# A decoder layer on one core: six tile banks, stepwise output products and a third norm by halves for the last chunk

## The chip, the cores and the metric

The kernel runs on one core of one Trainium2 chip. The metric is the device time of one execution in microseconds (us). TensorE (PE in the profile) multiplies matrices into PSUM, which has eight banks; VectorE (DVE), ScalarE (ACT) and GpSimd (POOL) do elementwise work; SyncE (SP) issues most DMA transfers. Engines run their own instruction lists in order and wait for each other on semaphores.

## The reference

The input is `x`, 16 sequences of 256 tokens of width 256, and a context of the same shape. Three sublayers follow each other, each as `x = layernorm(x + sublayer(x))`:

1. A recurrent attention: an input projection, a causal convolution over four steps, gates, cosine and sine of scaled values, a running sum over the tokens, a normalisation by head and an output projection.
2. An autocorrelation attention over the context: Fourier transforms of queries, keys and values, the five strongest lags by a softmax, the values shifted by those lags, an output projection.
3. A mixture of 8 experts in two branches:

```python
xV = einsum('btd,kdr->btkr', Q_side, V)
yW = einsum('btd,kdr->btkr', K_side, W)
prod = xV * cumsum(yW, axis=1)
weights = softmax(gelu(Q_side @ router_w1.T + b1) @ router_w2.T + b2)
out = einsum('btkr,kdr->btd', prod * weights[..., None], U) + weights @ b
out = out / n_valid[None, :, None]
```

The two branches are added, one with a factor, multiplied by `W_O`, and the third layer norm ends the layer.

## The kernel before

The 16 sequences are worked off in 8 chunks of two (512 tokens, four row blocks `q` of 128). Each chunk goes through three stages, named by their first letter: `a_...`, `b_...` and `c_...` are the steps of sublayers 1, 2 and 3. Every step is a small function on each engine that takes part in it, and every engine has a list of calls, written out in order, in which steps of up to three neighbouring chunks are interleaved: while chunk `i` is in stage a, chunk `i-1` is in b and `i-2` in c. The last chunk's stage c therefore runs alone. Before the first chunks, and among them, 34 `fold(k)` steps on PE and ACT combine weights.

PSUM banks are divided among the stages: 0 to 2 for a, 3 and 4 for b, 5 to 7 for c (`BANK_A`, `BANK_B`, `BANK_C`). Before a step writes a bank, `free_c` makes PE wait until the bank's former contents are read.

Stage c works over `NJ` = 8 expert tiles `j`. For each, `c_running(j)` (bank 5), `c_own(j)` (bank 6) and `c_spread(j)` (bank 7) are products on PE of nine instructions together; ACT copies the first to `cs`; DVE multiplies it by the spread weights (`c_scale`, L2810) and by the own product (`c_prod`, L2818), which gives `prod[:, j]`. When all eight are there, `c_out(n)` for each half `n` of the row blocks multiplies `prod` by `up` (L797) and adds the bias (L798): 64 instructions and 4. DVE adds the residual for each half and takes statistics (`c_residual`, L2827, L2608), aggregates them for all four row blocks after the second half (L2614); POOL makes scale and offset (`rstd`, L2309 to L2314, the `pow` in L2312), ACT applies them (`c_layer`, L1651) and writes into a part of `prod`, and SP stores the chunk (L371, 512 KB).

On PE, `a_factor(i, h)` (L557) needs `pair` from a chain over DVE and ACT that begins with `a_squares(i)` (L605). `b_transform` is L637, `b_wt` L674, `b_wf` L685, `a_project` L576, `a_sums` L593, `fold` L436 and L453; `a_conv` on DVE is L2490. SP's loads wait for PE steps: `load_residual(i)` for `b_transform(i-1, "xf", 1)`.

## Time and profile before

| | |
|---|---|
| three runs | 960.15, 957.73 and 961.58 us, median 960.15 |
| profiled execution | 960.6 us, span of its trace 958.7 us |
| PE busy | 865.2 us, 90% of the span |
| DVE busy | 766.4 us, 80% |
| ACT busy | 537.6 us, 56% |
| POOL busy | 96.2 us, 10% |
| mean granted TensorE clock | 0.957 of 2.4 GHz |

The span runs from the first to the last instruction or transfer of the profiled execution. The granted clock is the share of full speed that TensorE was given. An engine's busy share is a mean over the whole span.

### The profile page before, as it was taken

Reading aid. Unit: us, or ns where it says so; the run is one execution under the profiler, and the core shown is the slowest. Engines: PE = TensorE matmul, PEld = TensorE weight load, DVE = VectorE, ACT = ScalarE, POOL = GpSimd, SP = SyncE. Lnnn points to the kernel's source line nnn. Section 1 sums busy time; section 2 is a strip of 40 time slices with the busy share of each in tenths; the row PEclk is TensorE's granted clock in tenths of the full one; section 3 lists DMA queues with packets and bytes.
Section 4 is the critical chain, followed back from the end, with each engine's and each line's share of the span. In section 5 each row is a group of like instructions: output and inputs, shape, how many; then the busy total and the mean of one; then the engine's idle time right before and its main releaser. Section 6 shows DMA issues by size and latency. Waiting matters only on the chain.

```text
span 958.7 us, 11672 instructions
## 1 busy us (share of the span) xinstructions
PE 865.2 (90%) x4056; PEld 510.3 (53%) x4056; DVE 766.4 (80%) x1290; ACT 537.6 (56%) x875; POOL 96.2 (10%) x174
## 2 busy tenths in 40 slices
PE   3569865999999999999999999999999999997896
PEld 1134633663665556564756466555655475656345
DVE  5796888989878999899979997899879995373231
ACT  3484892677448673767467755856475655311310
POOL 2010011300120011100210011100200021001000
PEclk9679996999999999999999999999999999999898
DMA  9742034110432024100611044001510150000000
GB/s 292 133 89 44 6 83 88 46 45 0 83 72 67 0 48 85 66 23 13 120 45 45 1 91 107 23 0 35 120 44 1 23 111 23 1 1 23 0 1 22
DMA packets 41214, 50.81 MB, mean 53 GB/s; under 512 B 14843, under 2 KB 34374, under 8 KB 41158
## 3 DMA queue, kind: packets, MB, share of 16 engines
q0 software_dynamic: 7008, 25.21, 13.9%
q1 hardware_dynamic: 34006, 24.48, 8.9%
q8 instruction: 33, 0.54, 0.2%
q10 hardware_dynamic: 144, 0.39, 0.1%
q14 instruction: 23, 0.19, 0.1%
HBM read 20.68 MB, written 4.19 MB: 26 GB/s over the span
## 4 chain that ended last, share of the span: by engine, by line
PE 71%; DVE 18%; ACT 6%; issue 3%; POOL 1%; DMA 1%; ACTq 0%; DVEq 0%; SPq 0%; POOLq 0%
PE ps L797 12%; PE ps L778 10%; PE ps L769 9%; PE ps L653 6%; PE ps L593 5%; PE ps L735 5%; PE ps L576 4%; DVE sc L2569 3%; PE ps L623 3%; PE ps L712 3%; PE ps L637 3%; DVE zc L2490 2%; PE ps L436 2%; DVE sc L2561 2%; PE ps L702 2%
## 5 line engine op out<-in xcount | busy, mean ns | idle before, releaser
L2569 DVE TENSOR_TENSOR_SCAN sc<-mask,sc 128x1024 f32<-128x1024 bf16 x64 | 146.2, 2284 | 0.4
L778 PE MATMUL ps<-x2t,mv 128*128 128x512 f32 x256 | 123.7, 606 | 0.3 <-DVE prod L2818 0.3
L769 PE MATMUL ps<-cum,mw 128*128 128x512 f32 x256 | 122.1, 599 | 0.3 <-ACT cs L1646 0.2
L797 PE MATMUL ps<-up,prod 128*128 128x256 f32 x512 | 115.6, 381 | 1.3 <-DVE prod L2818 1.2
L797 PEld LDWEIGHTS ps<-up,prod 128*128 128x128 f32 x512 | 94.7, 190 | 18.9 <-issue 4.8
L2325 POOL DMA_DIRECT2D acc<-sq x48 | 42.1, 877 | 567.9 <-ACT sq L1552 567.9
L1646 ACT ACTIVATE cs<-ps 128x512 f32<-128x512 f32 x64 | 38.0, 594 | 99.8 <-PE ps L769 95.0
L2561 DVE TENSOR_TENSOR sc<-sc,g 128x1024 f32<-128x1024 f32 x64 | 77.3, 1208 | 7.4 <-ACT sc L1536 7.3
L2490 DVE SCALAR_TENSOR_TENSOR zc<-ps,cst,zc 128x510 f32<-128x510 f32 (+2 forms) x96 | 71.3, 742 | 13.7 <-ACT zc L1463 11.4
L769 PEld LDWEIGHTS ps<-cum,mw 128*128 128x128 f32 x256 | 47.4, 191 | 63.6 <-issue 59.5
L593 PE MATMUL ps<-sc,wy 64*64 64x512 f32 x512 | 66.1, 638 | 10.9 <-DVE sc L2569 10.9
L778 PEld LDWEIGHTS ps<-x2t,mv 128*128 128x128 f32 x256 | 47.0, 191 | 52.0 <-issue 44.1
L1552 ACT ACTIVATE sq<-sc 128x1024 f32<-128x1024 f32 x48 | 50.5, 1051 | 39.2 <-DVE sc L2569 22.9
L576 PE MATMUL ps<-xt,win 128*128 128x512 f32 x128 | 64.9, 636 | 7.1 <-DVE zc L2490 7.1
L2810 DVE TENSOR_TENSOR cs<-cs,ps 128x512 f32<-128x512 f32 x64 | 43.5, 679 | 30.2 <-ACT cs L1646 17.2
L735 PE MATMUL ps<-x2t,mr 128*128 128x512 f32 x128 | 59.3, 614 | 0.8 <-ACT x2t L1606 0.8
L1399 ACT ACT_TABLE_LOAD x45 | 57.7, 1283 | 2.0 <-PEq L3514 1.2
L2818 DVE TENSOR_TENSOR prod<-cs,ps 128x512 f32<-128x512 f32 x64 | 43.7, 683 | 12.6 <-PE ps L778 11.5
L1518 ACT ACTIVATE hq<-zc,cst 128x512 int32<-128x512 f32 x64 | 45.9, 719 | 7.4 <-DVE zc L2490 6.2
L2541 DVE SCALAR_TENSOR_TENSOR frac<-zc,cst,hq 128x512 f32<-128x512 f32 x64 | 47.5, 745 | 1.1 <-ACT hq L1518 0.7
L1536 ACT ACTIVATE sc<-hq,quarter 128x512 f32<-128x512 f32 x64 | 45.4, 709 | 0.0
L1651 ACT ACTIVATE prod<-x,rsc 128x256 f32<-128x256 f32 x32 | 16.6, 588 | 48.8 <-POOL rsc L2314 48.8
(263 smaller groups left out, 1478.1 us busy)
## 6 DMA issues: line engine op xcount, KB each, us to landing
acc<-sq POOLq DMA_DIRECT2D x48, 512.0 KB, 4.6
xa<-in_x_dram SPq DMA_DIRECT2D x8, 512.0 KB, 4.4
xs_a<-in_x_dram SPq DMA_DIRECT2D x8, 512.0 KB, 3.6
cin<-in_ctx_dram SPq DMA_DIRECT2D x8, 512.0 KB, 4.6
out_dram<-prod SPq DMA_DIRECT2D x8, 512.0 KB, 3.0
win<-in_in_proj_dram SPq DMA_DIRECT2D x1, 544.0 KB, 6.6
prod<-in_L_ffn_V_fwd_dram SPq DMA_DIRECT2D x2, 256.0 KB
prod<-in_L_ffn_W_fwd_dram SPq DMA_DIRECT2D x2, 256.0 KB
```

The lines of the kernel that those rows point to most:

```text
L576: last = mm(o, win[:, t, j * P:(j + 1) * P], xt[:, t, :], start=(t == 0), stop=(t == DT - 1))
L593: last = mm(ps[dst, BANK_A[("Y", r)], :], wy[src, 1 - c, m, :], sc[src, (2 * m + h) % 4, c, :], start=(m == 0 and c == 0), stop=(m == M - ...
L653: last = mm(o[:, b * D:(b + 1) * D], spec[:, first + t, c:c + P], w[:, t, :], start=(t == 0), stop=(t == DT - 1 and not biased))
L735: last = mm(o, mr[:, t, br, r * P:(r + 1) * P], x2t[:, t, :], start=(t == 0), stop=(t == 1))
L769: last = mm(o, mw[:, t, br, c:c + P], cum[:, t, :], start=(t == 0), stop=(t == 1))
L778: last = mm(o, mv[:, t, br, c:c + P], x2t[:, t, :], start=(t == 0), stop=(t == 1))
L797: mm(d, prod[:, j, q * P:(q + 1) * P], up[:, j, :], start=(j == 0), stop=False)
L1399: act.preload_act_table_set(name)
L1552: A(dst, sc[:, u % 4, :, :], ACT.Square, scale=1.0 / math.sqrt(2.0 * HD * M))\
L2490: STT(o[:, :, s:L], z[:, :, 0:L - s], cw[:, j, tap:tap + 1], o[:, :, s:L], ALU.mult, ALU.add)\
L2561: TT(sc[:, s, :, :], sc[:, s, :, :], g[:, h, :].unsqueeze(1).broadcast_to([P, 2, T]), ALU.mult)\
L2569: V.tensor_tensor_scan(flat, mask[:, 0:2 * T], flat, 0.0, ALU.mult, ALU.add)\
```

## The change

For the last chunk alone, the expert tiles alternate between two sets of three banks: 5, 6, 7 for even `j` and 3, 4, 2 for odd `j` (`BANK_LAST`); its outputs stand in banks 0 and 1. A new step `c_last(j)` adds tile `j`'s part to all four output blocks, for `j` from 0 to 6; `c_out` then does only tile 7 and the bias. `c_last(7, 0)` stands behind `c_spread(7, 1)`, the other six behind the last `c_own`.

For all chunks the third norm is done by halves: aggregates behind each half of the residual, `c_rstd(i, n)` on POOL, `c_layer(i, n)` on ACT and two stores of 256 KB. A few semaphores are merged under common names, with the same waits (`pr`, `ws`). Finally the lists of calls of PE, ACT, DVE and SP are in another order in many places of all chunks. The diff, cut to its core:

```diff
-POOL_C = Steps("pool_c", each("rstd", range(4)))
+POOL_C = Steps("pool_c", each("rstd", range(8)))
...
+BANK_LAST = dict(BANK_C)
+for _j in range(1, NJ, 2):
+    BANK_LAST.update({("c", _j): 3, ("x", _j): 4, ("w", _j): 2})
+BANK_LAST.update({("out", 0): 0, ("out", 1): 1})
...
-            def store(i):
-                sp.wait_ge(*ACT_C.at(i, "norm", NQ - 1))
-                sp.dma_start(rows(out, i), xs_c[:, :, :]).then_inc(stored, 16)
+            def store(i, n):
+                sp.wait_ge(*ACT_C.at(i, "norm", 2 * n + 1))
+                sp.dma_start(rows(out, i)[:, 2 * n:2 * n + 2, :], xs_c[:, 2 * n:2 * n + 2, :]).then_inc(stored, 16)
...
-            store(3)
+            store(3, 0)
+            store(3, 1)
+            load_x(7)
             load_ctx(6)
-            load_x(7)
+            store(4, 0)
+            store(4, 1)
             load_residual(6)
-            store(4)
             load_residual(7)
...
             def free_c(i, *name):
-                prev, i = before(BANK_C, i, name)
-                if prev is None:
-                    return ps[:, BANK_C[name], :]
+                bank = bank_c(i)[name]
+                o = ps[:, bank, :]
+                mine = [g for g in bank_c(i) if bank_c(i)[g] == bank]
+                n = mine.index(name)
+                if n:
+                    prev = mine[n - 1]
+                elif is_first(i) or bank < 5:
+                    return o
+                else:
+                    prev, i = [g for g in BANK_C if BANK_C[g] == bank][-1], i - 1
...
+            def accumulate(o, q, j, start):
+                return mm(o[:, (q % 2) * D:(q % 2 + 1) * D], prod[:, j, q * P:(q + 1) * P], up[:, j, :], start=start, stop=False)
+
+            @staged
+            def c_last(i, j):
+
+                o = [free_c(i, "out", n) for n in range(2)] if j == 0 else [ps[:, bank_c(i)[("out", n)], :] for n in range(2)]
+                pe.wait_ge(*VEC_C.at(i, "prod", j))
+                for q in range(NQ):
+                    last = accumulate(o[q // 2], q, j, j == 0 and q % 2 == 0)
+                last.then_inc(*PE_C.tick("last", j))
+
             @staged
             def c_out(i, n):
-                o = free_c(i, "out", n)
+                o = ps[:, bank_c(i)[("out", n)], :] if is_last(i) else free_c(i, "out", n)
                 pe.wait_ge(*VEC_C.at(i, "prod", NJ - 1))
                 if is_first(i):
                     pe.wait_ge(placed, 16 * PARTS)
                 for q in range(2 * n, 2 * n + 2):
-                    d = o[:, (q % 2) * D:(q % 2 + 1) * D]
-                    for j in range(NJ):
-                        mm(d, prod[:, j, q * P:(q + 1) * P], up[:, j, :], start=(j == 0), stop=False)
-                    last = mm(d, wparts[:, q * P:(q + 1) * P], bp3[:, 0, :], start=False, stop=True)
+                    for j in (range(NJ - 1, NJ) if is_last(i) else range(NJ)):
+                        accumulate(o, q, j, j == 0)
+                    last = mm(o[:, (q % 2) * D:(q % 2 + 1) * D], wparts[:, q * P:(q + 1) * P], bp3[:, 0, :], start=False,
+                              stop=(q % 2 == 1 or not is_last(i)))
                 last.then_inc(*PE_C.tick("out", n))
...
-            fold(0)
             a_project(0, 3)
             a_sums(0, 0)
+            fold(0)
             fold(1)
-            a_sums(0, 1)
             fold(2)
             fold(3)
             fold(4)
             fold(5)
             fold(6)
+            a_sums(0, 1)
             fold(7)
...
             b_transform(0, "cf", 0)
             b_transform(0, "cf", 1)
+            a_project(1, 3)
             b_transform(0, "xf", 0)
             b_transform(0, "xf", 1)
-            a_project(1, 3)
             b_spectrum(0, "qa")
...
+            c_last(7, 1)
+            c_last(7, 2)
+            c_last(7, 3)
+            c_last(7, 4)
+            c_last(7, 5)
+            c_last(7, 6)
             c_out(7, 0)
             c_out(7, 1)
...
-            def c_layer(i):
-                ln_apply(i, 2, x2, xs_c, ACT_C, POOL_C)
+            def c_layer(i, n):
+                if n == 0 and not is_last(i):
+                    act.wait_ge(*PE_C.at(i, "out", 1))
+                act.wait_ge(*POOL_C.at(i, "rstd", 4 * n + 3))
+                for q in range(2 * n, 2 * n + 2):
+                    A(xs_c[:, q, :], x2[:, q, :], ACT.Identity, bias=rs[2][:, 2, q:q + 1], scale=rs[2][:, 1, q:q + 1])\
+                        .then_inc(*ACT_C.tick("norm", q))
...
+            @staged
+            def c_rstd(i, n):
+
+                q, sums = slice(2 * n, 2 * n + 2), rs[2]
+                pool.wait_ge(*VEC_C.at(i, "aggr", 2 * n + 1))
+                G.tensor_tensor(sums[:, 0, q], mvr[2][:, q, 1], eps_[:, q], ALU.add).then_inc(*POOL_C.tick("rstd", 4 * n))
+                G.tensor_tensor(sums[:, 2, q], mvr[2][:, q, 0], minus[:, q], ALU.mult).then_inc(*POOL_C.tick("rstd", 4 * n + 1))
+                pool.wait_ge(*POOL_C.at(i, "rstd", 4 * n + 1))
+                G.tensor_tensor(sums[:, 1, q], sums[:, 0, q], half_[:, q], ALU.pow).then_inc(*POOL_C.tick("rstd", 4 * n + 2))
+                pool.wait_ge(*POOL_C.at(i, "rstd", 4 * n + 2))
+                G.tensor_tensor(sums[:, 2, q], sums[:, 2, q], sums[:, 1, q], ALU.mult).then_inc(*POOL_C.tick("rstd", 4 * n + 3))
...
                 ln_stats(i, 2, x2, VEC_C, n)
-                if n == 1:
-                    ln_aggr(i, 2, VEC_C)
+                dve.wait_ge(*VEC_C.at(i, "stats", 2 * n + 1))
+                V.tensor_copy(seen[:, 2:3], st[2][:, 2 * n, 0:1])
+                for q in range(2 * n, 2 * n + 2):
+                    V.bn_aggr(mvr[2][:, q, :], st[2][:, q, :]).then_inc(*VEC_C.tick("aggr", q))
```

Other moves in the lists that matter below: on PE folds 20 and 21 go from before `a_factor(0, 0)` to behind `a_project(1, 1)`; between `b_wt(1)` and `b_wf(1)`, neighbours before, four steps are put; in chunk 3 `b_out(2, 1)` goes from before to behind `a_factor(3, 0)`; in chunk 4 `b_transform(4, "cf", 0)` goes from before to behind `a_factor(4, 0)`; in chunk 6 the order `a_squares`, `b_transform(6, "cf", 0)`, `a_factor(6, 0)` becomes `a_squares`, `b_out(5, 1)`, `a_factor(6, 0)`, `b_transform(6, "cf", 0)`. On ACT folds are moved as well: fold 0 to behind `a_turns(0, 6)`, folds 8 and 9 before `a_angles(0, 7)`, fold 10 behind it. On DVE `b_fold(0, "xf")` goes from behind `a_conv(1, 1)` to behind `a_conv(1, 2)`.

## Rows read from the trace of the kernel before

**Rows 1.** The page, busy us by engine (share of the span) x instructions.
```profile
PE 865.2 (90%) x4056; PEld 510.3 (53%) x4056; DVE 766.4 (80%) x1290; ACT 537.6 (56%) x875; POOL 96.2 (10%) x174
```

**Rows 2.** Windows: stretch, length, busy us of each engine, granted clock, DMA share, GB/s.
```profile
168.00:880.00 712.00, 696.70 (x3354) 417.85 (x3351) 611.98 (x1037) 417.92 (x672) 75.03 (x128) 0.99 0.20 45
880.00:907.50 27.50, 17.96 (x49) 7.84 (x48) 6.47 (x19) 12.27 (x20) 1.64 (x5) 0.81 0.06 19
907.50:933.80 26.30, 26.19 (x64) 11.34 (x64) 10.32 (x15) 4.58 (x8) 0.00 (x0) 1.00 0.00 1
933.80:949.30 15.50, 14.50 (x68) 12.24 (x68) 2.37 (x6) 0.00 (x0) 0.00 (x0) 1.00 0.00 0
949.30:958.70 9.40, 0.00 (x0) 0.00 (x0) 2.01 (x9) 2.07 (x4) 1.56 (x4) 0.62 0.17 56
```

**Rows 3.** Timeline of the end: start, us, engine, instruction, [idle before it <- releaser].
```profile
908.77 0.69 DVE L2818 TENSOR_TENSOR prod<-cs,ps 128x512 f32<-128x512 f32 x1
909.78 0.38 PE L786 MATMUL ps<-wparts,sel 128*128 128x512 bf16 x1
...
933.88 0.69 DVE L2818 TENSOR_TENSOR prod<-cs,ps 128x512 f32<-128x512 f32 x1 [0.68 <-PE ps L778]
934.71 3.69 PE L797 MATMUL ps<-up,prod 128*128 128x256 f32 x16 [0.94 <-DVE prod L2818]
...
949.24 0.88 DVE L2827 SCALAR_TENSOR_TENSOR x<-ps,cst,x 128x256 f32<-128x256 f32 x2 [5.47 <-PE ps L798]
951.01 0.37 DVE L2614 BATCH_NORM_AGGREGATE mvrc<-stc 128x2 f32<-128x6 f32 x4
951.46 0.20 POOL L2309 TENSOR_TENSOR rsc<-mvrc,eps_ 128x4 f32<-128x4 f32 x1 [67.67 <-DVE mvrc L2614]
951.89 1.01 POOL L2312 TENSOR_TENSOR rsc<-rsc,half_ 128x4 f32<-128x4 f32 x1
953.21 2.07 ACT L1651 ACTIVATE prod<-x,rsc 128x256 f32<-128x256 f32 x4 [20.74 <-POOL rsc L2314]
955.31 0.37 SPq L371 DMA_DIRECT2D out_dram<-prod  x1
```

**Rows 4.** DMA issues: tensors, queue, count, KB each, median us to landing.
```profile
out_dram<-prod SPq DMA_DIRECT2D x8, 512.0 KB, 3.0
bp<-bp POOLq DMA_DIRECT2D x2, 16.0 KB, 1.9
```

**Rows 5.** PE's waits, 185 to 880 us: us in total, times, longest us.
```profile
PE ps L557 <- DVE pair L2590: 2.8, 2, 2.4
...
PE ps L637 <- DVE cin L2635: 1.9, 1, 1.9
PE ps L685 <- ACT wtt L1594: 1.2, 1, 1.2
...
PE ps L769 <- ACT cs L1646: 0.2, 1, 0.2
```

**Rows 6.** Timeline of PE at two of these waits.
```profile
240.37 1.05 PE L685 MATMUL ps<-wtt,fdft 128*128 128x32 f32 x8 [1.24 <-ACT wtt L1594]
...
796.34 0.47 PE L557 MATMUL ps<-pair,spreads 128*128 128x256 f32 x2 [2.37 <-DVE pair L2590]
```

**Rows 7.** Windows of 4 us behind these two waits, columns as in rows 2.
```profile
240.00:244.00 4.00, 3.63 (x12) 2.21 (x13) 2.66 (x8) 0.71 (x3) 0.95 (x1) 0.70 0.58 112
...
798.00:802.00 4.00, 4.00 (x16) 3.36 (x15) 1.54 (x3) 2.48 (x3) 0.00 (x0) 0.58 0.00 0
```

**Rows 8.** Timeline of the start: PE and DVE.
```profile
55.47 3.69 PE L593 MATMUL ps<-sc,wy 64*64 64x512 f32 x16 [10.70 <-DVE sc L2569]
...
115.07 2.29 DVE L2490 SCALAR_TENSOR_TENSOR zc<-ps,cst,zc 128x510 f32<-128x510 f32 x3
117.76 1.88 PE L576 MATMUL ps<-xt,win 128*128 128x512 f32 x4
120.49 2.31 DVE L2490 SCALAR_TENSOR_TENSOR zc<-ps,cst,zc 128x510 f32<-128x510 f32 x3 [3.13 <-ACT zc L1463]
```

More of the change, by code:

```diff
@@ L832, in _ @@
             fold(19)
+            a_sums(0, 2)
             a_sums(0, 3)
             a_squares(0)
-            fold(20)
-            fold(21)
             a_factor(0, 0)
@@ L909, in _ @@
             b_transform(1, "xf", 1)
+            a_spread(2, 1)
+            a_project(2, 2)
             c_weights(0)
-            a_project(2, 2)
-            c_spread(0, 0)
             b_spectrum(1, "qa")
@@ L931, in _ @@
             c_spread(0, 4)
-            a_sums(2, 0)
+            b_wt(1)
             c_own(0, 4)
@@ L936, in _ @@
             c_own(0, 5)
+            b_wf(1)
             c_running(0, 6)
             c_spread(0, 6)
-            b_wt(1)
-            b_wf(1)
             c_own(0, 6)
             c_running(0, 7)
-            a_sums(2, 1)
+            a_sums(2, 0)
             c_spread(0, 7)
             c_own(0, 7)
+            a_sums(2, 1)
             b_back(1)
@@ L992, in _ @@
             c_running(1, 2)
+            a_sums(3, 0)
             c_spread(1, 2)
@@ L1008, in _ @@
             c_spread(1, 6)
+            a_sums(3, 1)
             c_own(1, 6)
-            b_wt(2)
             c_running(1, 7)
             c_spread(1, 7)
+            b_wt(2)
             c_own(1, 7)
@@ L1046, in _ @@
             a_spread(4, 1)
+            a_project(4, 2)
             c_own(2, 0)
@@ L1138, in _ @@
             c_running(3, 4)
+            a_sums(5, 0)
+            b_wt(4)
             c_spread(3, 4)
-            b_wt(4)
             c_own(3, 4)
             c_running(3, 5)
+            b_wf(4)
             c_spread(3, 5)
-            b_wf(4)
             c_own(3, 5)
@@ L1170, in _ @@
             a_scores(6)
+            a_project(6, 0)
             a_out(5, 1)
+            c_transpose(4, 0)
+            c_transpose(4, 1)
+            a_project(6, 1)
             c_hidden(4, 0)
-            a_project(6, 0)
-            a_project(6, 1)
             c_hidden(4, 1)
@@ L1194, in _ @@
             b_spectrum(5, "vb")
+            c_own(4, 0)
+            c_weights(4)
             a_project(6, 3)
+            c_spread(4, 0)
             c_running(4, 1)
+            a_sums(6, 0)
+            b_corr(5)
             c_spread(4, 1)
@@ L1212, in _ @@
             c_spread(4, 5)
+            b_wf(5)
             c_own(4, 5)
@@ L1215, in _ @@
             c_spread(4, 6)
-            b_wf(5)
+            a_sums(6, 1)
             c_own(4, 6)
@@ L1225, in _ @@
             a_sums(6, 2)
+            a_sums(6, 3)
             b_out(5, 0)
+            a_squares(6)
             b_out(5, 1)
-            a_sums(6, 3)
-            a_squares(6)
+            a_factor(6, 0)
             b_transform(6, "cf", 0)
-            a_factor(6, 0)
             b_transform(6, "cf", 1)
             a_factor(6, 1)
+            a_transpose(7, 0)
+            a_transpose(7, 1)
+            a_out(6, 0)
+            a_scores(7)
+            a_out(6, 1)
+            a_project(7, 0)
             c_transpose(5, 0)
             c_transpose(5, 1)
-            a_transpose(7, 0)
-            a_out(6, 0)
-            a_transpose(7, 1)
-            a_out(6, 1)
-            a_scores(7)
-            a_project(7, 0)
             a_project(7, 1)
@@ L1268, in _ @@
             c_own(5, 1)
+            a_sums(7, 0)
             c_running(5, 2)
@@ L1271, in _ @@
             c_own(5, 2)
-            a_sums(7, 0)
             c_running(5, 3)
-            b_wt(6)
             c_spread(5, 3)
@@ L1277, in _ @@
             c_running(5, 4)
+            c_spread(5, 4)
+            b_wt(6)
+            c_own(5, 4)
             b_wf(6)
-            c_spread(5, 4)
-            c_own(5, 4)
             c_running(5, 5)
@@ L1367, in _ @@
             c_spread(7, 1)
+            c_last(7, 0)
             c_own(7, 1)
@@ L1697, in _ @@
             a_turns(0, 6)
-            a_squares(0, 2)
-            a_angles(0, 5)
-            a_turns(0, 7)
-            a_squares(0, 3)
+            fold(0)
             fold(1)
@@ L1704, in _ @@
             fold(3)
+            a_squares(0, 2)
+            a_angles(0, 5)
             fold(4)
@@ L1708, in _ @@
             fold(7)
+            a_turns(0, 7)
+            a_squares(0, 3)
             a_angles(0, 6)
@@ L1943, in _ @@
             a_project(4, 0)
+            a_project(4, 1)
+            b_transform(3, "cf", 0)
             c_hidden(2, 0)
-            a_project(4, 1)
-            a_turns(4, 0)
-            b_transform(3, "cf", 0)
             c_hidden(2, 1)
@@ L2085, in _ @@
             a_scores(6)
+            b_layer(4)
+            b_transform(5, "cf", 0)
+            b_transform(5, "cf", 1)
             a_exp(6)
             a_project(6, 0)
+            c_transpose(4, 0)
+            c_transpose(4, 1)
             c_hidden(4, 0)
+            a_project(6, 1)
             a_layer(5)
-            a_project(6, 1)
             c_hidden(4, 1)
@@ L2892, in _ @@
             a_conv(1, 2)
+            b_fold(0, "xf")
             a_conv(1, 3)
@@ L3303, in _ @@
             a_den(7)
+            b_fold(6, "xf")
             a_conv(7, 1)
```

681 lines of the change are left out of this document (345 added, 336 removed).

## The prediction

> **What bounds the kernel now.** I read the page's busy shares first [rows 1]: TensorE (PE) is busy for 865.2 of 958.7 us, VectorE (DVE) for 766.4. A share is an average over stages, so I cut the span into stretches [rows 2]. From 168 to 880 us, where chunks overlap, PE is busy 696.70 of 712 us and DVE 611.98: there PE sets the pace, and 15.3 us of its time are open. From 880 to 907.5 us the last chunk is alone; PE works 17.96 of 27.5 us at a mean granted clock of 0.81, waiting for a chain of norm, gates and softmax. Then come the last chunk's expert tiles, 907.5 to 933.8 us, with PE busy 26.19 of 26.3 us; the output products, 14.50 us of PE work in a stretch of 15.5 us; and 9.4 us with no PE work at all. The rows of the end [rows 3] show one gap of 0.94 us, where PE waits for the last `prod`, and behind the last product a serial chain: residual and statistics on DVE, four small operations on POOL, four activations on ACT (2.07 us), one store.
>
> The profiled execution took 960.6 us, 1.9 us more than its span and 0.45 us more than the median of the three runs (960.15). The sum is made against 960.6 us, and its result shifted by that 0.45 us.
>
> **Six tile banks.** With three banks the next tile's products must wait until ACT or DVE has read the bank. In this stretch they do not: the 26.19 of 26.3 us leave 0.11 us for all waits [rows 2]. Alternating banks 5, 6, 7 with 3, 4, 2 therefore gains between nothing and 0.1 us; I take nothing. What hides the reads is the time that PE takes for a tile: 64 instructions at nine a tile are seven tiles, 3.7 us each, against two DVE operations of 0.69 us [rows 3]. The banks below 5 were used by chunk 7's first two stages, which are over before.
>
> **Output products as tiles come.** The same 64 product and 4 bias instructions are issued in another order; at 14.50 us for all, a bias counting half, a product instruction is 0.22 us [rows 2]. `c_last(7, 0)` stands behind `c_spread(7, 1)` and needs `prod` 0, which DVE ends at 908.77 + 0.69 = 909.46 us, while the spread begins only at 909.78 us [rows 3]: it does not wait. It pushes what is behind it by eight instructions, 1.8 us, which come off the end again. `c_last(7, 1)` to `c_last(7, 6)` stand behind the last tile's own product; their `prod` tiles are made by then, and their 48 instructions, 10.5 us, cover the 0.94 us in which PE waited for `prod` 7 [rows 3]. PE's last product ends 0.94 us earlier, at about 948.2 us. If that cover failed, the cost is the same 0.94 us.
>
> **Third norm and store by halves.** Since all outputs grow in step, the first half is ready only 1.1 us before the second: four products and two biases, five times 0.22 us. That is 947.1 us. DVE takes for the second half with all four aggregates from 949.24 to 951.01 + 0.37 = 951.38 us, 2.14 us [rows 3], and two aggregates less are 0.18 us less: 1.96 us a half. Half 0 keeps DVE until 949.1 us, so half 1 begins then and not at 948.2 us when PE is done, and ends at 951.05 us against 951.38. Of the 0.94 us, 0.6 are given back: the split makes DVE the queue at the end. This item is -0.3 us.
> POOL's four operations reach from 951.46 to 953.2 us, of them the `pow` on four columns 1.01 us [rows 3]. No row shows one on two columns: its cost lies between 0.5 us (by columns) and 1.01 us (all fixed). Its neighbours need 0.20 us for as many numbers, so most of any such operation is fixed; I take 1.01 us and no gain. Half 0 leaves POOL at 950.9 us, before half 1 comes. ACT then has two activations behind POOL's last result where it had four: 2.07 us become 1.05, a gain of 1.0 us.
> The last store carries 256 KB, not 512. From its issue at 955.31 us to the end of the span are 3.4 us [rows 3], 3.0 of them landing; a copy of 16 KB took 1.9 us [rows 4]. Half the data lies between 1.9 and 3.0 us; half way it is 2.45 us, a gain of 0.55 us. SP's issue of the first half's store (0.37 us) lies beside ACT's work, 2 us ahead.
> In the other seven chunks the halves cost one more copy and one more wait on DVE (0.15 us), four more POOL operations and one more issue on SP. DVE has 100 us open between 168 and 880 us [rows 2], so some 1 us for seven chunks is hidden; if DVE were the bound it would be paid.
> The tail's sum is -0.3 - 1.0 - 0.55 = -1.85 us. Its bounds are -2.9 us (short `pow`, 1.9 us landing) and -1.0 us (only ACT's part comes).
>
> **The lists of calls.** The diff also moves calls on every engine in all chunks; most of the uncertainty is here.
> In the start folds 2 to 6 move into PE's wait of 10.70 us before the second `a_sums(0, ...)` [rows 8]. What ends these stages is DVE's and ACT's work, so shorter PE queues pay little, and ACT's copies move too: fold 10 comes behind `a_angles(0, 7)` and holds PE's `mv` folds back. I take nothing for both. A later place pays: `a_project(1, 3)` moves ahead of the two `xf` transforms, and `b_fold(0, "xf")` into DVE's 3.13 us idle behind `a_conv(1, 2)`. PE may begin the projection when that convolution ends, at 115.07 + 2.29 = 117.36 us, not at 117.76 [rows 8]. I take -0.6 us for the start, with -3.1 us (the whole idle) and +2 us (the later copies) as ends.
> In the middle PE has 13.9 us of waits in 14 groups, of which four are shown, the first and the last among them [rows 5]. Two can be pointed at: `b_wt` and `b_wf` of chunk 1 stood next to each other (1.2 us) and get four steps between them, and `b_transform(6, "cf", 0)` waited 1.9 us for the fold of `cin` and now stands behind `b_out(5, 1)` and `a_factor(6, 0)`. Together -3.1 us. Against that, in chunks 3 and 4 less work stands before `a_factor`, which waits on a chain over DVE and ACT: 2.4 us where nothing fills it [rows 6]. And `load_residual(6)` now queues on SP behind both stores of chunk 4; if it came late, `a_residual(6, 0)` would hold PE. I take +2.1 us for these, -1.0 us together, with -7 us (half the waits go) and +6 us as ends.
> A wait costs more than its length. In the four microseconds that hold the end of the 1.2 us wait the granted clock is 0.70, and behind the wait of 2.4 us it is 0.58, so PE spent part of them at 1.2 instead of 2.4 GHz [rows 6, 7]. The second took 0.42 of 4 us, 1.7 us, beside the gap. Over 712 us the mean clock of 0.99 is some 7 us [rows 2].
> The Trainium skill (TensorE: Matmul & The Clock Gate, HAM oscillation) says that it is long idle gaps of TensorE that throttle it. By that rule gaps of one or two microseconds cost only their length, and the first rival below would end at 962.5 us, no measurable change; the trace does not agree, with its 0.58 behind a gap of 2.4 us, and the measurement decides.
>
> **Sum.** 960.6 - 1.85 - 0.6 - 1.0 = 957.15 us for the profiled execution, 956.7 as a median: I say 957.
>
> **Rivals.**
> A, slower: new gaps at the seams between chunks, where `a_factor` waits for DVE's `pair`. One more gap like that of chunk 7 costs 2.4 + 1.7 = 4.1 us [rows 6, 7], and two of them 8.2 us: 960.15 - 2.45 + 8.2 = 966 us. It decides from two gaps on. For it: chunk 4 has nothing left between `a_squares` and `a_factor`. Against: chunk 4 waited there before as well, and chunk 6 gets a filler. 0.09.
> B, clearly better lists: half of the middle's 13.9 us of waits and half of its 7 us of clock go, 10.5 us, less 3 us of new ones; the start gives twice its 0.6 us. With the tail it is 960.15 - 7.5 - 1.2 - 1.85 = 949.6 us. For it: the two waits above go with their clock. Against: PE is at 97.9% there already. 0.21.
> C, the change does not do what it says: queueing at DVE takes the whole 0.94 us, the store lands no sooner, and the lists cancel out; 959.2 us. For it: 0.6 us are given back in my own sum. 0.18.
> My forecast has 0.52, with 954 to 960 us as its own range.
>
> **How the numbers follow.** About 0.5% (4.8 us) is what a measurement of this kernel can tell from no change: faster begins below 955.35 us, slower above 964.95. Faster gets B and the lower edge of the forecast (0.09), 0.30; slower gets nearly all of A, 0.08; no change the rest, 0.62. The range cuts off A and half of B: 951.5 to 962 us.
>
> **What would show it.** 56 product instructions in one run behind the last tile, without a gap before `c_out(7, 0)`; the second half's residual starting when DVE is free, not when PE is done; two activations behind POOL's last result; a last store that lands in about 2.45 us; PE's end 8.6 us before the span's, where it was 9.5. In the middle PE's waits sum to 11 to 15 us. I am wrong if that sum is below 8 or above 18 us, if the first `c_transpose` moves by over 2 us, or if the first `c_last` waits.

## The result: 0.9% faster, and the profile after

The changed kernel took 951.16 us (median of five executions) against 961.28 us for the kernel before beside it, a ratio of 0.9913 with a 95% interval of 0.9889 to 0.9937. A second timing on another occasion gave 952.25 against 959.41 us, 0.9926 [0.9907, 0.9945]. Both are faster by more than the 0.5% bound. The forecast was 957 us: the first median lies 0.3 us below the low end of its range, the second inside it, and both are below the forecast's own range of 954 to 960. The prediction had put 0.62 on no measurable change and 0.30 on faster. One execution each of `tail_only`, `lists_only` and `after_order` below took 2009 to 2288 us; the ratios leave them out.

The page of after begins with its span and the busy shares:

```profile
span 948.8 us, 11724 instructions
PE 858.4 (90%) x4056; PEld 507.4 (53%) x4056; DVE 767.0 (81%) x1298; ACT 538.2 (57%) x876; POOL 106.4 (11%) x206
```

PE is busy for 6.8 us less than before with the same products [rows 1]. Next, the windows of after, columns as in [rows 2]:

```profile
180.00:872.00 692.00, 676.70 (x3293) 405.48 (x3292) 601.70 (x1020) 415.78 (x666) 79.86 (x146) 1.00 0.20 45
...
899.80:926.10 26.30, 26.29 (x70) 12.56 (x71) 9.63 (x14) 4.48 (x8) 0.00 (x0) 1.00 0.00 1
926.10:940.00 13.90, 13.89 (x64) 11.09 (x62) 2.40 (x5) 0.06 (x1) 0.00 (x0) 1.00 0.00 0
940.00:948.80 8.80, 0.00 (x0) 0.00 (x0) 2.74 (x12) 2.18 (x4) 2.48 (x8) 0.68 0.18 60
```

The first window of [rows 2] begins 12 us earlier in the work, at 168 us. The stretch of before that has the same 3293 instructions of PE is this:

```profile
180.00:879.00 699.00, 684.16 (x3293) 409.43 (x3292) 601.07 (x1013) 413.50 (x663) 70.05 (x118) 0.99 0.20 44
```

The middle has 15.3 us without PE work after (692.00 - 676.70) and 14.8 us before (699.00 - 684.16). The waits have not gone, they have moved. The three largest groups of waits between 180 and 875 us, by line (busy, mean ns, idle time ahead and its releasers):

```profile
L765 PE MATMUL ps<-x2t,mr 128*128 128x512 f32 x112 | 49.8, 593 | 1.6 <-ACT prod L1663 1.6
...
L667 PE MATMUL ps<-fdft,cin 128*128 128x128 f32 x112 | 14.6, 277 | 1.5 <-DVE x L2826 1.5
...
L587 PE MATMUL ps<-pair,spreads 128*128 128x256 f32 x48 | 12.4, 339 | 7.5 <-DVE pair L2672 4.7 <-issue 1.8 <-DVE zc L2680 0.8
```

L587 is the old L557: now two factor spreads, those of chunks 4 and 7, wait 2.4 us each, where one did [rows 5, 6]. So one of the two new waits that rival A asked for did come, in chunk 4. What is different is the clock behind such waits. These are the windows of after that hold the two waits of 2.4 us:

```profile
476.00:480.00 4.00, 1.63 (x15) 0.99 (x14) 2.95 (x11) 1.81 (x5) 2.35 (x4) 1.00 0.00 0
480.00:484.00 4.00, 3.57 (x28) 3.24 (x27) 2.55 (x4) 2.60 (x6) 0.00 (x0) 1.00 0.02 6
788.00:792.00 4.00, 1.88 (x15) 1.83 (x16) 3.26 (x7) 3.22 (x7) 0.80 (x2) 1.00 0.01 3
792.00:796.00 4.00, 3.25 (x17) 2.52 (x16) 3.85 (x5) 2.37 (x3) 0.00 (x0) 1.00 0.00 0
```

The granted clock is 1.00 behind both, where before had 0.58 behind the same wait [rows 7]. The end of after, the rows that answer to [rows 3] (PE's weight loads left out):

```profile
927.29 10.96 PE L819 MATMUL ps<-up,prod 128*128 128x256 f32 x50
...
939.72 0.27 PE L839 MATMUL ps<-bp,wparts 128*128 128x256 bf16 x1
...
940.71 0.24 DVE L2915 BATCH_NORM_AGGREGATE mvrc<-stc 128x2 f32<-128x6 f32 x2
940.86 0.84 DVE L2909 SCALAR_TENSOR_TENSOR x<-ps,cst,x 128x256 f32<-128x256 f32 x2
...
942.60 0.24 DVE L2915 BATCH_NORM_AGGREGATE mvrc<-stc 128x2 f32<-128x6 f32 x2
942.92 0.20 POOL L2372 TENSOR_TENSOR rsc<-mvrc,eps_ 128x2 f32<-128x2 f32 x1 [0.50 <-DVE mvrc L2915]
...
943.34 0.70 POOL L2375 TENSOR_TENSOR rsc<-rsc,half_ 128x2 f32<-128x2 f32 x1
...
944.35 1.09 ACT L1721 ACTIVATE prod<-x,rsc 128x256 f32<-128x256 f32 x2 [0.80 <-POOL rsc L2377]
```

The products run in one piece, without a wait for the last `prod`. PE ends at 939.99 us; the second half's residual starts only at 940.86 us, when DVE has finished the first half. Behind POOL's last result stand two activations. From PE's end to the span's end are 8.8 us, where there were 9.5.

What ends last is no longer the store. The page's row for the stores (KB each, median us to landing) and the closing instructions of after, each with its duration in ns and its start in us:

```profile
out_dram<-prod SPq DMA_DIRECT2D x16, 256.0 KB, 2.1
...
L186 POOLq EVENT_SEMAPHORE  x2: 17/17/17, 948.6 to 948.7; - x2
...
L186 POOLq DRAIN  x1: 4479/4479/4479, 944.1 to 944.1; - x1
...
L186 SPq COMPARE_BRANCH  x1: 33/33/33, 947.6 to 947.6; - x1
```

and the same instructions of before:

```profile
L171 POOLq EVENT_SEMAPHORE  x2: 17/17/17, 958.5 to 958.6; - x2
...
L171 POOLq DRAIN  x1: 4482/4482/4482, 952.9 to 952.9; - x1
...
L171 SPq COMPARE_BRANCH  x1: 33/33/33, 958.3 to 958.3; - x1
```

The `COMPARE_BRANCH` is the end of SyncE's wait for the last landing; the `DRAIN` closes GpSimd's list and begins at the end of its `pow`. Before, the drain was over at 957.42 us and the store landed at 958.27 us, so the store came last. After, the store landed at 947.61 us and the drain was over only at 948.56 us, so the drain came last. The other profiles agree: in all seven with the whole store the span ends 0.39 us behind the landing, in all six with halves 0.24 us behind the drain.

### The profile page after: what moved, and what is told of

Read it like the earlier page. It is cut to its first block, busy times and chain, and to the rows that moved or that the text cites. A ratio compares the mean times of both kernels' runs of the same rounds, so it can differ in the third digit from the quotient of the medians.

```text
span 948.8 us, 11724 instructions
## 1 busy us (share of the span) xinstructions
PE 858.4 (90%) x4056; PEld 507.4 (53%) x4056; DVE 767.0 (81%) x1298; ACT 538.2 (57%) x876; POOL 106.4 (11%) x206
## 4 chain that ended last, share of the span: by engine, by line
PE 72%; DVE 17%; ACT 6%; issue 3%; DMA 1%; POOL 1%; ACTq 0%; DVEq 0%; SPq 0%; POOLq 0%
PE ps L819 12%; PE ps L808 10%; PE ps L799 10%; PE ps L683 7%; PE ps L623 5%; PE ps L765 5%; PE ps L606 4%; PE ps L653 3%; DVE sc L2651 3%; DVE zc L2572 2%; PE ps L742 2%; PE ps L667 2%; PE ps L732 2%; DVE sc L2643 1%; PE ps L774 1%
## 5 line engine op out<-in xcount | busy, mean ns | idle before, releaser
L808 PE MATMUL ps<-x2t,mv 128*128 128x512 f32 x256 | 121.8, 598 | 0.2 <-DVE prod L2900 0.2
L606 PEld LDWEIGHTS ps<-xt,win 128*128 128x128 f32 x128 | 24.2, 204 | 35.4 <-issue 22.2
```

What stands on the lines that cost most here:

```text
L606: last = mm(o, win[:, t, j * P:(j + 1) * P], xt[:, t, :], start=(t == 0), stop=(t == DT - 1))
L808: last = mm(o, mv[:, t, br, c:c + P], x2t[:, t, :], start=(t == 0), stop=(t == 1))
```

## The experiments

Each kernel was timed beside the kernel before on the same chip, whose median in the three batches was 959.74, 959.41 and 959.34 us. PE runs a 128x256 product call of fp32 as two instructions of 0.22 us, so a filler call is 0.44 us.

### One part at a time

`tail_only` is the changed kernel with the lists of before: every call that both have stands where it stood before.

```diff
             c_spread(7, 1)
+            c_last(7, 0)
...
             c_own(7, 7)
+            c_last(7, 1)
...
+            c_last(7, 6)
             c_out(7, 0)
...
-            store(7)
+            store(7, 0)
+            store(7, 1)
```

> The kernel before with the change's last chunk alone: six banks, output products as tiles come, third norm and stores by halves in all chunks; the calls that both versions share stay in the order of before. Theory one (the tail and the lists are separate items, the tail worth what the two profiles show from the first last-chunk spread to the end of the span, 51.14 against 48.99 us): 2.1 us faster than before, a ratio of 0.998, with the low granted clock at 240 and 798 us still there. Rival (the halves, through two stores and more operations in every chunk, are what keeps the clock up in the middle): 8 to 10 us faster, ratio 0.990 to 0.992, and no low clock in the middle.

`lists_only` is the reverse: the structure of before with the order of after.

> The kernel before with the lists of calls of after alone: three banks, output products at the end, third norm and store whole. Theory one: the lists are worth the 7.1 us by which the middle is shorter in the profile of after, plus 0.7 us of clock in the first hidden products of the last chunk: 7 to 8 us faster, ratio 0.992, the middle without low granted clock. Rival: with the tail as before nearly nothing of it comes, under 3 us, ratio over 0.997.

`tail_only` took 957.38 us, ratio 0.998 [0.9961, 0.9999], 1.9 us faster. `lists_only` took 955.78 us, 0.9956 [0.9938, 0.9973], 4.2 us faster. Multiplied they give 0.9936, inside the intervals of both timings of after: the parts add up, and the lists carry about two thirds. Neither rival holds. But `lists_only` stays short of the expected 7 to 8 us, which came from one profile of before held against one of after. The signs in the profiles came by halves: `tail_only` has the low clock at the wait of chunk 7 and not at the wait of 1.24 us, and the middle of `lists_only` is not free of it, it lies behind the wait of 2.37 us of chunk 4 (480 us).

### Is the low clock a property of the order?

> The kernel before, unchanged, for a second profile. If the low clock follows from the order of work, the granted clock is 0.70 or near it again in 240 to 244 us, 0.68 in 280 to 284, 0.77 to 0.81 in 690 to 698 and 0.58 in 798 to 802, at the same instructions to within 0.1 us. If the low clock falls by chance, it lies at other instructions or is missing, and the first transpose of the last chunk's stage c (886.01 us) moves by over 2 us.

This is a second profile of the unchanged kernel before, at the four places where the first had low clock: the two of [rows 7], of which the second now comes 2.1 us earlier, 280 to 284 us (0.68 in the first) and 692 to 696 us (0.57):

```profile
240.00:244.00 4.00, 3.43 (x12) 2.06 (x13) 2.86 (x8) 0.91 (x3) 0.95 (x1) 0.78 0.51 97
280.00:284.00 4.00, 4.00 (x19) 2.44 (x20) 3.86 (x14) 0.99 (x2) 0.80 (x3) 1.00 0.13 43
...
692.00:696.00 4.00, 3.90 (x25) 3.23 (x25) 1.86 (x3) 2.06 (x4) 0.00 (x0) 1.00 0.01 2
792.00:796.00 4.00, 1.77 (x12) 1.81 (x13) 3.26 (x6) 3.22 (x7) 0.91 (x2) 0.90 0.05 17
796.00:800.00 4.00, 4.00 (x18) 3.50 (x17) 1.52 (x3) 2.48 (x3) 0.00 (x0) 0.67 0.00 0
```

Two of the four drops are there again, two are not, although the same waits (1.24, 1.85 and 2.37 us) stand in the trace at the same instructions. The first transpose of the last chunk's stage c came 2.3 us earlier (883.70 us). So the same program loses different amounts to the clock in different executions; the 29 executions of before in this batch spread from 955.9 to 961.8 us. The profile on which the prediction stands was one of the dearer ones.

### Filling the waits

`before_fill` puts useless products into two waits:

```diff
+            def filler(o, n):
+                for _ in range(n):
+                    mm(o[:, 0:L], fdft[:, 0, 0:P], fdft[:, 0, :], start=True, stop=True)
...
                 o = free_a(i, "fe", h)
+                if i in (7,) and h == 0:
+                    filler(o, 10)
...
                 o = free_b(i, "wf")
+                if i == 1:
+                    filler(o, 5)
```

> The kernel before, with two of its waits on TensorE filled by products whose result is overwritten: ten of 128x256 ahead of the first factor spread of chunk 7 (wait of 2.37 us), five ahead of the second weight transform of chunk 1 (wait of 1.24 us). Nothing of the reference's work is left out. If it is the waits that bring the low clock, the filled stretches keep the full clock: 240:244 and 798:802 at 1.00 where they were 0.70 and 0.58, and 1.7 plus 1.8 us come back, 3.5 us faster, ratio 0.9964. If the low clock has another cause, it stays or moves and the time is the same or up to 0.3 us longer.

It took 960.27 us, 1.0006 [0.9992, 1.0021]. The filler was twice too long, because a call is two instructions: 6.6 us of products in 3.6 us of waits, 3.0 us too many. In its profile both filled stretches have the full clock, and the only low clock in the middle stands behind the unfilled wait of 1.85 us. Standing still in spite of the surplus means that some 2.4 us came back, but that is an inference from two terms, so the experiment was made again with the right sizes: five calls at chunk 7, three at chunk 1 and four at the wait of 1.85 us of chunk 6.

> The kernel before with three waits filled by products of 0.44 us whose result is overwritten: three before the second weight transform of chunk 1 (wait of 1.24 us), four before the first context transform of chunk 6 (1.85 us), five before the first factor spread of chunk 7 (2.37 us). Nothing of the reference's work is left out. Theory one: low clock at these three places never comes; it came there five times in the two profiles of before, 1.7 us each, so the mean falls by 3 to 4.5 us, ratio 0.9955 to 0.997, and the spread between executions shrinks. Rival (the low clock has another cause than these waits): it shows up elsewhere in the middle, ratio 1.000.

956.37 us, 0.9974 [0.9959, 0.9989]: 2.5 us faster by doing more work. The twelve executions spread over 3.9 us, the 17 of before beside them over 6.0. In its profile the former places of low clock:

```profile
240.00:244.00 4.00, 4.00 (x17) 2.08 (x15) 3.83 (x9) 0.11 (x1) 0.77 (x1) 1.00 0.69 131
688.00:692.00 4.00, 3.90 (x30) 3.38 (x29) 2.66 (x4) 3.46 (x7) 0.00 (x0) 1.00 0.01 2
792.00:796.00 4.00, 3.24 (x25) 2.88 (x24) 2.66 (x4) 2.82 (x6) 0.00 (x0) 1.00 0.00 0
```

With the three waits filled no low clock is left anywhere in the middle of this profile. So it is these waits that bring the low clock, and filling them is worth 2.5 us on the mean (by the interval 1.1 to 3.9). The expectation had 3 to 4.5 us; the last fillers end some 0.3 us later than the waits did, which takes a part.

The same was done to after, five calls at each of its two waits of 2.4 us (`i in (4, 7)`).

> The kernel after with its two waits of 2.4 us (first factor spread of chunks 4 and 7) filled by five overwritten products of 0.44 us each. Nothing of the reference's work is left out. Theory one: as the waits sometimes bring the low clock, filling them gains on the mean up to 2 us against after, ratio to before 0.989 to 0.991, and a narrower spread. Rival (order of after is free of low clock anyway): the same time as after within 0.5 us.

951.58 us, 0.9923 [0.9905, 0.9942], against 0.9926 for after itself. No gain shows, as the rival had it; the intervals would not rule out the theory's smaller gains.

### Does the order or the moment decide?

> The kernel after, unchanged, timed again with a second profile. Theory one (a wait of 1.2 us or more on TensorE brings the low clock in some executions and not in others; each costs about 1.7 us; the first profile of after had none in the middle, that of before four): the times spread over some 6 us as those of before do, their median is 952 to 956 us, the ratio to before 0.993 to 0.996, and this profile has low clock behind at least one of the waits at 479, 500, 583 and 790 us. Rival (the order of after doesn't bring the low clock): times within 2 us of 951, ratio 0.991, full clock behind all four waits again.

The median was 952.25 us and six executions lay between 949.9 and 952.8 us, all within 2 us of 951 as the rival had it. The profile has again full clock behind all four waits, the rival's other sign. `after_shift` delays all that follows by five filler calls, 2.2 us:

```diff
                 o = free_c(i, "h", n)
                 pe.wait_ge(*ACT_C.at(i, "xT", 1))
+                if i == 0 and n == 0:
+                    filler(o, 5)
```

> The kernel after with five overwritten products of 0.44 us each ahead of the first hidden product of chunk 0, so that all later work comes 2.2 us later and each later wait falls at another moment. Nothing of the reference's work is left out. If only the order of work counts: 2.2 us slower than after, with the same clock. If the moment at which a wait falls decides on the low clock within a run: 2.2 us slower plus 0 to 5 us, with low clock behind one or more of the waits that had none in the profile of after.

955.51 us, 0.9956 [0.9939, 0.9972], 3.3 us above after in the same batch, of which 2.2 are the filler. The 1.1 us beyond it are hardly more than these intervals can tell; the profile says more. The order of work is that of after; in its profile the clock is low at two places, not at the wait of chunk 7:

```profile
276.00:280.00 4.00, 2.66 (x12) 2.30 (x13) 3.32 (x6) 0.55 (x1) 1.25 (x4) 0.79 0.00 0
280.00:284.00 4.00, 4.00 (x19) 2.67 (x18) 3.79 (x14) 0.81 (x3) 1.11 (x3) 0.79 0.44 133
480.00:484.00 4.00, 1.63 (x11) 0.99 (x12) 2.82 (x10) 1.84 (x5) 2.35 (x4) 0.89 0.00 0
484.00:488.00 4.00, 4.00 (x27) 4.00 (x27) 2.75 (x4) 2.57 (x6) 0.00 (x0) 0.69 0.00 0
...
796.00:800.00 4.00, 3.25 (x21) 2.78 (x20) 3.83 (x4) 2.58 (x4) 0.00 (x0) 1.00 0.00 0
```

So the order alone does not keep the clock up: the wait of chunk 4 had full clock in both profiles of after and has not here. Part of what after gained in the clock is not tied to its order. The same edit was made to before.

> The kernel before with five overwritten products of 0.44 us each ahead of the first hidden product of chunk 0, so that later waits fall 2.2 us later; the same edit made after 3.4 us slower on the mean, of which 2.2 us are the products. Nothing of the reference's work is left out. If the moment at which a wait falls decides on the low clock within a run, the cost here differs from there and may lie anywhere from -2 to +5 us, with low clock at other waits than the four of before's profile (240, 278, 692 and 796 us). If the order of work alone decides: 2.2 us slower, low clock at the same waits.

960.84 us, 1.0016 [1.0, 1.0033]: 1.5 us slower, while the same edit cost after 3.3 us; the interval (0 to 3.2 us) holds the 2.2 us added as well. In this profile the waits of 1.24 us (242.51 us) and 1.85 us (690.00 us) have full clock behind them. The one at chunk 7 hasn't; PE's rows there, with the idle time in brackets:

```profile
794.50 0.76 PE L557 MATMUL ps<-pair,spreads 128*128 128x256 f32 x2 [2.37 <-DVE pair L2596]
795.06 1.91 PE L641 MATMUL ps<-fdft,cin 128*128 128x128 f32 x8
```

and the same two instructions in the profile of after:

```profile
790.12 0.47 PE L587 MATMUL ps<-pair,spreads 128*128 128x256 f32 x2 [2.38 <-DVE pair L2672]
790.43 1.05 PE L667 MATMUL ps<-fdft,cin 128*128 128x128 f32 x8
```

Same work, same wait: 0.76 and 1.91 us at the lower of TensorE's two levels (1.2 GHz), 0.47 and 1.05 us at the upper (2.4 GHz).

In the first profiles of before and after and in those of the experiments (`after_order`, below, left out) there are 43 waits of 1.2 to 2.4 us on PE between 180 and 880 us. With the lists of before low clock stands behind 12 of 25, with those of after behind 2 of 18. They are not alike: with the lists of before it stands behind the wait of 1.24 us in three of five profiles, behind that of 1.21 us (482 us) in none of seven, behind that of 1.85 us in three of seven; with those of after behind the 2.37 us of chunk 4 in two of four and behind those of 1.60 and 1.22 us in none of ten. The wait at chunk 7 has it in six of six profiles with the lists of before where it wasn't filled, and in none of four with those of after. That much does depend on the order. Which part of the order does it was not tried; what differs is that the lists of before have another wait of 1.85 us some 105 us ahead of it, and those of after none of 1.2 us for 200 us. Whether that plays a part is not shown.

### One of the two waits pointed at

`before_move` does one of the moves named in the prediction:

```diff
             b_wt(1)
-            b_wf(1)
             c_own(0, 6)
+            b_wf(1)
```

> The kernel before with the own product of chunk 0's tile 6 moved between the two weight transforms of chunk 1, into the wait of 1.24 us at 240 us. Theory one: the wait goes, and with it the low clock that stood there in two of three profiles with this wait: 1.2 plus about 1.2 us on the mean, ratio 0.9975. Rival (the wait's length comes back at the next thing that ends late, and the low clock falls elsewhere): 0 to 0.5 us, ratio over 0.9995, and the first squares of chunk 2 (272.93 us) no more than 0.5 us earlier.

957.52 us, 0.9986 [0.9974, 0.9998], 1.3 us faster, between theory and rival, and the interval excludes neither. The wait of 1.24 us became another:

```profile
239.71 1.98 PE L778 MATMUL ps<-x2t,mv 128*128 128x512 f32 x4 [0.93 <-DVE prod L2818]
```

The product moved forward now waits for DVE to read its bank. In length 0.3 us are gained. The clock in 240 to 244 us was 1.00 here, and 0.70 and 0.78 in the two profiles of before. The first squares of chunk 2 began at 270.61 us, 2.3 us earlier than in the first profile of before, of which 1.7 us are that clock; the rival allowed 0.5 us.

### The end of the kernel

`halves_only` has the third norm and the stores by halves, and neither the six banks nor the new order of products:

```diff
 def bank_c(i):
-    return BANK_LAST if is_last(i) else BANK_C
+    return BANK_C
...
-                    for j in (range(NJ - 1, NJ) if is_last(i) else range(NJ)):
+                    for j in range(NJ):
...
-                if n == 0 and not is_last(i):
+                if n == 0:
                     act.wait_ge(*PE_C.at(i, "out", 1))
```

> The kernel before with the third norm and the stores by halves alone, in all chunks: three banks, output products at the end, lists of before. The first half's output is ready 7 us before the second's, so DVE has no queue. Theory one (the terms add up): behind TensorE's end 0.2 us less on DVE, 0.3 on GpSimd, 1.0 on ScalarE and 0.06 at the store, so 9.5 us from TensorE's end to the span's end become 7.9, while the wait of 0.94 us for the last product tile stays: 1.6 us faster than before, ratio 0.9984. That is two thirds of the tail's 2.15 us from the halves alone. Rival (the halves pay only together with the products as tiles come): under 0.7 us.

956.79 us, 0.9978 [0.9962, 0.9995], as much as `tail_only` within the intervals. In its profile the second half's residual begins 0.04 us after PE's end, there is no queue:

```profile
948.78 0.27 PE L839 MATMUL ps<-bp,wparts 128*128 128x256 bf16 x1
949.09 0.88 DVE L2902 SCALAR_TENSOR_TENSOR x<-ps,cst,x 128x256 f32<-128x256 f32 x2 [5.12 <-PE ps L839]
...
951.60 0.70 POOL L2368 TENSOR_TENSOR rsc<-rsc,half_ 128x2 f32<-128x2 f32 x1
...
952.60 1.09 ACT L1714 ACTIVATE prod<-x,rsc 128x256 f32<-128x256 f32 x2 [2.42 <-POOL rsc L2370]
```

From PE's end (949.05 us) to the span's end (957.05 us) are 8.0 us, expected 7.9. Here too GpSimd's drain ends last (956.82 us, the store lands at 955.85 us). The halves alone shorten this part by 1.5 us; together with the products as tiles come it is 0.65 us, and PE's end comes earlier instead.

`after_order` tries to have both, by letting the first half end 2.8 us ahead:

```diff
-            c_last(7, 5)
-            c_last(7, 6)
+            c_last(7, 5, 0)
+            c_last(7, 6, 0)
             c_out(7, 0)
+            c_last(7, 5, 1)
+            c_last(7, 6, 1)
             c_out(7, 1)
```

> The kernel after, with the second half's products of tiles 5 and 6 behind the first half's last products: the first half then ends 2.8 us ahead of the second instead of 1.1 us, more than the 1.9 us that DVE takes for a half. If it is the queue at DVE that gave back 0.6 of the 0.94 us: the time from TensorE's end to the end of the aggregates falls from 2.85 to 2.0 us, TensorE's end stays where it is, and the kernel is 0.8 us faster than after, ratio to before 0.991 to 0.992. Rival (DVE's own work for the second half has grown, the queue is not it): no change there, 2.8 us again.

952.24 us, 0.9923 [0.9904, 0.9942], the same as after (0.9926); a gain of 0.8 us is below what these intervals can tell. Its profile is of the execution of 2146 us, in which PE's products took about twice as long, so only the distances between DVE's operations are read from it:

```profile
2136.51 0.88 DVE L2912 SCALAR_TENSOR_TENSOR x<-ps,cst,x 128x256 f32<-128x256 f32 x2 [4.10 <-PE ps L840]
...
2138.28 0.24 DVE L2918 BATCH_NORM_AGGREGATE mvrc<-stc 128x2 f32<-128x6 f32 x2
```

The residual waits for PE (4.10 us), and from its start the half takes 2.01 us, so DVE's own work for it has not grown. That there is no queue says little here, as PE was slow. What shows the queue is `halves_only`: the same four kinds of operation end 2.04 us behind PE's end there, without a queue, and 2.85 us behind it in after, with one. That removing the queue makes the kernel faster is not shown.

## Why the prediction came out as it did

Here are the profiles side by side, all in us. "Middle" runs from the first to the last chunk's first `c_transpose`; "lost" is worked out from the windows of four microseconds in it with low clock, as (1 - clock) x 4 while PE has work; "tail, PE" runs from `c_running(7, 0)` to PE's last product, "end" from there to the last instruction of the trace.

| kernel | start | middle | lost | tail, PE | end |
|---|---|---|---|---|---|
| before | 180.07 | 705.94 | 6.8 | 48.26 | 9.46 |
| before_again | 180.28 | 703.42 | 3.4 | 48.26 | 9.47 |
| tail_only | 179.68 | 701.89 | 1.7 | 46.78 | 8.80 |
| halves_only | 179.62 | 703.98 | 3.3 | 49.88 | 8.00 |
| before_move | 179.73 | 702.97 | 3.4 | 48.26 | 9.45 |
| before_shift | 180.07 | 704.39 | 1.7 | 48.26 | 9.46 |
| lists_only | 180.84 | 699.70 | 1.6 | 49.91 | 9.45 |
| after | 179.99 | 698.99 | 0 | 46.79 | 8.81 |
| after_again | 179.46 | 699.04 | 0 | 46.79 | 8.80 |
| after_shift | 180.73 | 702.92 | 3.3 | 46.79 | 8.80 |

**The middle, -1.0 us: wrong in sum, and right at full clock only in the number.** Without what the clock took (and without the 2.2 us of filler in the two shifted kernels) the middle of these ten profiles is 699.1 to 700.7 us with the lists of before and 697.4 to 699.1 with those of after, 1.6 us less on the mean. But this is not the waits getting shorter, as the term had it. Some went, others came: PE's idle time for the same instructions is 14.8 us before and 15.3 us after. The waits listed as in [rows 5] sum to 14.9 us after, inside the 11 to 15 us named, and to 14.2 us before, where the prediction had 13.9. From the first to the last `c_transpose`, with the lost time taken off, PE is busy for 678.3 to 679.1 us in `before`, `before_again` and `tail_only` and for 677.2 to 677.7 us in `lists_only`, `after` and `after_again`, for the same 3294 instructions up to the last wait. So the gain at full clock lies in PE's busy time, for which the prediction had no term; which neighbours in the lists bring it was not tried. The larger step that failed is the one behind it. The prediction said that a wait costs more than its length and had the 7 us of clock in front of it, and then put -1.0 us for waits alone, as if the clock's part stayed as it was. The lists of before lose 3.4 us to it on the mean of six profiles, those of after 1.2 of four. The two together, 1.6 and 2.2, are the 3.8 us by which the middle is shorter on the mean (703.4 to 699.6), not 1.0. Rival B had the clock's half in its price, but by half of the waits going, and they did not. None of the three signs of being wrong came either: they looked at the waits and not at the clock behind them.

**One profile was taken for the kernel.** The profile of before lost 6.8 us to the clock in the middle and that of after nothing. Compared with each other they show 7 us where the means differ by 3.8. A range that took in this spread would have reached below 951.5 us.

**The start, -0.6 us: not gained.** The first `c_transpose` stands at 179.5 to 180.8 us in all profiles; the five with the lists of after have a mean of 180.35 us, the eight with those of before (the two filled ones with it) 179.87. The 0.5 us between them are within what single profiles of one kernel differ by (179.99 and 179.46 us for after). What was worth taking (`a_project(1, 3)` at the end of the convolution) was lost again: that projection began at 117.83 us after, 117.76 before [rows 8]. All five profiles with the new lists have low clock at 84 to 92 us, none of the eight others; in after it follows a new wait of 2.37 us before `a_factor(0, 0)` that ends at 83.95 us, where folds 20 and 21 stood before. That it accounts for the 0.5 us was not tested.

**The products as tiles come.** PE's part of the tail became 1.47 us shorter (48.26 to 46.79), not 0.94. The wait for the last `prod` is gone, as said. Another 0.29 us go between the first and second `c_spread` (2.22 to 1.93 us): before, the second `c_running` stood 0.40 us behind the first spread, because ACT had not read its bank, and now 0.21. That is the six banks' worth, taken as 0 to 0.1. The remaining 0.24 us are left unassigned. DVE's queue gave back 0.67 us: from PE's end to the last aggregate were 2.18 us and are 2.85, and the prediction's times (948.2 and 951.05 us) have the same 2.85. This step is right.

**What no term had: low clock inside the tail.** In four of the eight profiles whose products stand at the end, PE's part takes 49.9 instead of 48.26 us; in none of the five with the new tail. This is the row of `lists_only` behind the two short waits for the softmax, against 1.88 us for the same four products in after:

```profile
903.18 3.62 PE L769 MATMUL ps<-cum,mw 128*128 128x512 f32 x4
```

Whether the new tail avoids it or was lucky five times is open. By four of eight it would be worth 0.8 us.

**The halves: the terms came, and the end did not follow them.** ACT's part is 1.09 instead of 2.07 us, as predicted. POOL's `pow` on two columns took 0.70 us, not 1.01: of the bounds 0.5 and 1.01 I took the wrong end, and with the wait ahead of them the four operations gained 0.33 us. The last store landed 2.14 us after its issue (955.31 to 958.27 us before is 2.96), so the landing term of 0.55 us measured 0.82. Yet the end hardly followed: from ACT's end to the span's end are 3.38 us before and 3.36 after. Before, the span ended 0.39 us after the landing. At that distance after would have ended at 948.00 us; it ended at 948.80, 0.24 us behind GpSimd's drain. So the step that failed here is the path: the sum takes the store for the last thing in the kernel, and GpSimd's drain has no term in it. It costs 0.8 us (an estimate from these two distances). The gains on GpSimd and at the landing, 0.33 and 0.27 us beyond their terms, pay for most of it, so that 8.8 us came near the 8.6 predicted by luck.

**The tail in sum** was -1.85 us and measured -2.12 (57.72 to 55.60 us from `c_running(7, 0)` on), without the low clock. `tail_only` at -1.9 us confirms it.

**The reckoning.** Start +0.5, middle -3.8, tail with its clock -1.47 - 0.8 - 0.65, and -0.4 for the last chunk between its transpose and `c_running(7, 0)` (14.7 us on the mean of the six profiles with the lists of before and without filler, 14.4 of the five with the new lists), make -6.6 us; the second timing has 7.2 us, and the rest is within the intervals. The first timing has 10.1 us because the kernel before took 961.28 us beside it, against 959.3 to 959.7 us in the three later batches. So the forecast of 957 us was 5 to 6 us too high; 3.0 us of that are the clock, 2.2 in the middle and 0.8 in the tail.

**The clock rule.** The Trainium skill (TensorE: Matmul & The Clock Gate, HAM oscillation) would have waits of one or two microseconds cost their length only. The traces disagree, by 14 drops behind 43 waits of 1.2 to 2.4 us and by `before_fill2`. But that the low clock follows a wait always, as the prediction treated it in rival A, is wrong too.

## What to carry to other kernels

Before costing a wait of one or two microseconds on TensorE from one profile, take two or three profiles of the same kernel: the length of the wait repeats to a hundredth of a microsecond, the clock behind it doesn't, and where it falls it costs as much again. Count such waits and multiply by a chance and a price (here 12 of 25 over all of them, but from none of seven to six of six for a single one, about 1.7 us each) instead of reading the one that the trace happens to show. When the outputs of several blocks are made to grow in step, the blocks all become ready at the end, and the engine behind them queues: let one block finish ahead by at least the time that the next engine takes for it (here `halves_only` has 2.04 us behind PE's last product and after 2.85; that such an order pays was not shown). And when the last store is made shorter, look at what else closes the kernel: here GpSimd's drain, 4.48 us from its last `pow`, took over as the end.

## What was unexpected of the hardware

- The same wait of 2.37 us on TensorE ahead of the same instructions (chunk 7) left the granted clock at 1.00 in four profiles with the lists of after and took it to the half level in six with those of before.
- Low clock also stood twice where no single wait was longer than 0.8 us: behind 0.23 and 0.78 us within 1.5 us at 277 us in before, and behind two of 0.79 and 0.78 us in `after_shift`.
- Adding 12 useless products of 0.44 us into waits made a kernel of 959 us faster by 2.5 us (1.1 to 3.9 us).
- Moving all later work by 2.2 us cost one kernel 3.3 us and the other 1.5, each to within some 1.6 us.
- GpSimd's `pow` took 1.01 us for four columns and 0.70 us for two, while its add and multiply took 0.20 us for either.
- A store of 256 KB landed 2.1 us after its issue and one of 512 KB 3.0 us, but the kernel's end came only 0.02 us sooner behind ScalarE's last activation: GpSimd's closing `DRAIN` of 4.48 us held it.
